# Quantising two weight matrices in 2048-wide pieces instead of 1024-wide ones, with bf16 intermediates

## What is computed

```python
x = x + attention(layernorm(x), Wq, Wk, Wv, Wo, rel_emb)   # 16 heads of 64, relative bias
x = x + ffn(layernorm(x), w1, w2)

def quant_weight(w):                    # the part that the change touches
    s = clip(mean(abs(w)), 1e-5, None)
    return clip(round(w / s), -1, 1) * s
def ffn(x, w1, w2):                     # w1 4096 x 1024, w2 1024 x 4096, float32
    h = gelu(quant_act(x) @ quant_weight(w1).T)
    return quant_act(h) @ quant_weight(w2).T
```

## Time and profile before

| | us |
|---|---|
| median of 3 runs | 9136.47 |
| the profiled execution, its time | 9122.06 |
| its span on the slowest core (core 3) | 9120.5 |
| spans of the 8 cores | 9107.6 to 9120.5 |
| busy in that span: PE / DVE / ACT / POOL | 3183.0 / 2173.7 / 2030.0 / 85.1 |
| the chain that ended last: DMA / DVE / ACT / PE / issue of DMAs by SP | 21% / 19% / 19% / 15% / 12% |

### The profile page before, as it was taken

How to read it: one execution, slowest core, us unless ns; L and a number is a source line. 1 busy time by engine, 2 the same in 40 slices (tenths; PEclk the granted TensorE clock), 3 DMA queues, 4 the chain that set the end, 5 groups by cost and what they waited for, 6 DMA issues and landing times.

```text
span 9120.5 us, 47056 instructions; the slowest of 8 cores (9107.6 to 9120.5 us)
## 1 busy us (share of the span) xinstructions
PE 3183.0 (35%) x12444; PEld 1036.2 (11%) x12444; DVE 2173.7 (24%) x2480; ACT 2030.0 (22%) x2214; POOL 85.1 (1%) x164
## 2 busy tenths in 40 slices
PE   0000014767675100233225225676774000233155
PEld 0000001112121000011112101121211000111022
DVE  0334310000000156266600200000001364366400
ACT  0010102546452010022100004464550000122100
POOL 0000000000000000000000000000000000000000
PEclk9999997889887555666667667898886555666577
DMA  3323222000001400200032122000002301100222
GB/s 69 116 90 124 74 61 52 14 28 14 19 23 51 124 30 28 61 23 23 27 89 75 61 53 42 25 14 19 23 14 78 109 26 46 44 19 23 53 76 74
DMA packets 661831, 459.47 MB, mean 50 GB/s; under 512 B 546242, under 2 KB 579140, under 8 KB 653380
## 3 DMA queue, kind: packets, MB, share of 16 engines
q1 hardware_dynamic: 652868, 447.81, 17.0%
q0 software_dynamic: 8704, 8.66, 0.7%
HBM read 209.23 MB, written 143.79 MB: 39 GB/s over the span
## 4 chain that ended last, share of the span: by engine, by line
DMA 21%; DVE 19%; ACT 19%; PE 15%; SPq 12%; issue 7%; DVEq 5%; ACTq 2%; PEldq 0%; PEld 0%; POOL 0%; POOLq 0%
ACT AR L719 11%; SPq L103 9%; PE PS L970 5%; DMA ARF<-w_in 4%; DVEq L276 3%; PE PS L656 3%; DVE qst_b L290 3%; DVE qst_u L298 2%; DVE qst_c L285 2%; SPq L106 2%; ACT qst_t L933 2%; DVE AR L312 2%; ACT AR L902 2%; DVE stc_mcol L909 2%; DMA lnt<-yat_dram 1%
## 5 line engine op out<-in xcount | busy, mean ns | idle before, releaser
L896 PE MATMUL PS<-AR 128*128 128x512 bf16 x2016 | 507.2, 419 | 2416.8 <-DMA AR<-xq_dram 1541.5
L719 ACT ACTIVATE AR<-PS,neg40c 128x1024 bf16<-128x1024 f32 x1024 | 1140.2, 1113 | 374.4 <-issue 194.0
L970 PE MATMUL PS<-AR 128*128 128x512 bf16 x1984 | 457.0, 390 | 727.8 <-DMA AR<-hq_dram 666.8
L769 DVE RECIPROCAL ARF<-ARF 128x32 f32<-128x32 f32 x16 | 5.6, 353 | 2793.1 <-DMA ARF<-ARF 2793.1
L896 PEld LDWEIGHTS PS<-AR 128*128 128x128 bf16 x2016 | 210.8, 106 | 2713.4 <-issue 2521.9
L604 PE MATMUL PS<-AR 128*128 128x512 bf16 x448 | 142.9, 472 | 968.8 <-DMA AR<-wv_bf 908.3
L700 PE MATMUL PS<-AR 64*128 64x512 bf16 x1024 | 406.3, 397 | 117.9 <-DMA AR<-g_dram 117.9
L730 PE MATMUL PS<-AR 128*65 128x512 bf16 x1024 | 387.8, 379 | 165.1 <-ACTq L92 164.6
L708 PE MATMUL PS<-AR,j_sb 128*128 128x512 bf16 x1024 | 409.2, 400 | 0.0
L704 PE MATMUL PS<-AR 64*128 64x512 bf16 x1024 | 406.6, 397 | 0.0
L712 PE MATMUL PS<-AR,j_sb 128*128 128x512 bf16 x1024 | 399.0, 390 | 0.0
(11 more groups left out here) (111 smaller groups left out, 3536.1 us busy)
## 6 DMA issues: line engine op xcount, KB each, us to landing
ARF<-w_in SPq DMA_DIRECT2D x64, 512.0 KB
ARF<-w_in SPq DMA_DIRECT2D x32, 1024.0 KB
xtile<-x_in SPq DMA_DIRECT2D x64, 512.0 KB
hq_dram<-AR SPq DMA_DIRECT2D x32, 1024.0 KB
AR<-g_dram SPq DMA_DIRECT2D x32, 992.0 KB
x_dram<-x1t SPq DMA_DIRECT2D x32, 512.0 KB
xtile<-x_dram SPq DMA_DIRECT2D x32, 512.0 KB
xtile<-x_dram SPq DMA_DIRECT2D x64, 256.0 KB
```

The source lines that it names most:

```text
L719: E("scalar", lambda S, ewg=ewg, j=j: S.activation(out=ewg[:, 0:1024], in_=PS[:, 1024 * j:1024 * (j + 1)], func=AF.Exp, bias=neg40c[:], sc ...
L896: E("tensor", lambda T, tt=tt, dc=dc, hg=hg: T.matmul(ps[hg], xqT[dc][:, 128 * tt:128 * (tt + 1)], w1qT[dc][:, 512 * hg:512 * (hg + 1)], s ...
L970: T.matmul(ps[bk], hqT[hc][:, 128 * ttl:128 * (ttl + 1)], w2qT[hc][:, 512 * dg:512 * (dg + 1)], start=(hc == 0), stop=False))
```

## The change

In the second pass DVE works on 2048 columns at a time. The two comparisons write bf16 tiles (`qw_b0` and `qw_u0`, or `qw_b1` and `qw_u1`, in turn) instead of float32, and the difference is written in place over the first of them. A piece of w2 is then one part with one store. For w1, whose rows are 1024 long, two row blocks are laid side by side in a buffer (`RB` is 2), with two loads and two stores. This also holds for the first pass over w1: 16 reductions of 2048 instead of 32 of 1024, and `wsum` has one column per pair. A tile of 2048 ones (`ones2k`) is set at the start of the program. All new tiles lie in a part of the buffer `AR` that the stages after the barrier use otherwise. The work of `batch_program` is the same.

```diff
--- before.py
+++ after.py
@@ -262,7 +262,11 @@
         gselch = carve(0, NUM_BUCKETS, 512, F32)
         wchunk = carve(512, 128, 2048, F32)
         wchunk2 = carve(4096, 128, 2048, F32)
-        qst_o2 = carve(50944, 128, 1024)
+        qw_b0 = carve(0, 128, 2048)
+        qw_u0 = carve(2048, 128, 2048)
+        qw_b1 = carve(4096, 128, 2048)
+        qw_u1 = carve(6144, 128, 2048)
+        ones2k = carve(8192, 128, 2048)
 
         PS = es.enter_context(nc.psum_tensor("PS", [128, 4096], F32))
         ps = [PS[:, 512 * i:512 * (i + 1)] for i in range(8)]
@@ -320,6 +324,7 @@
         E("vector", lambda V: V.memset(onesrow[:], 1.0))
         E("vector", lambda V: V.memset(ones_big, 1.0))
         E("vector", lambda V: V.memset(onesr2k, 1.0))
+        E("vector", lambda V: V.memset(ones2k, 1.0))
         v0 = r.inc("vector", "V")
         r.dma("sync", "dS", j_sb[:], jmat_c)
         r.dma("sync", "dS", sel2_sb[:], sel2_c)
@@ -361,17 +366,27 @@
 
         wbufs = (wchunk, wchunk2)
         wbg = {0: None, 1: None}
-        obufs = (qst_o, qst_o2)
+        obufs = ((qw_b0, qw_u0), (qw_b1, qw_u1))
         obg = {0: None, 1: None}
         wq_state = {"g": 0, "o": 0}
 
         def wquant(w_src, w_dst, nrows, ncols, scol):
             CW = 2048 if ncols % 2048 == 0 else 1024
+            RB = 2048 // CW
             nch = nrows // 128
             ncc = ncols // CW
+            n_ig = nch // RB
+
+            def loads(buf, ch, cc):
+                for rb in range(RB):
+                    ld = r.dma("sync", "dS", buf[:, CW * rb:CW * (rb + 1)],
+                               w_src[128 * (ch + rb):128 * (ch + rb + 1),
+                                     CW * cc:CW * (cc + 1)])
+                return ld
+
             E("vector", lambda V: V.memset(wsum[:], 0.0))
             r.inc("vector", "V")
-            for ch in range(nch):
+            for ig in range(n_ig):
                 for cc in range(ncc):
                     bi = wq_state["g"] % 2
                     wq_state["g"] += 1
@@ -379,25 +394,24 @@
                     if wbg[bi]:
                         for sn_, v_ in wbg[bi]:
                             r.wait("sync", sn_, v_)
-                    ld = r.dma("sync", "dS", buf[:, 0:CW],
-                               w_src[128 * ch:128 * (ch + 1), CW * cc:CW * (cc + 1)])
+                    ld = loads(buf, RB * ig, cc)
                     r.wait("vector", "dS", ld)
-                    E("vector", lambda V, CW=CW, buf=buf: V.reduce_sum(
-                        stc["tmp"][:], buf[:, 0:CW], axis=mybir.AxisListType.X,
+                    E("vector", lambda V, buf=buf: V.reduce_sum(
+                        stc["tmp"][:], buf[:, 0:2048], axis=mybir.AxisListType.X,
                         apply_absolute_value=True))
                     VD()
...
                     vv = r.inc("vector", "V")
                     wbg[bi] = [("V", vv)]
             E("vector", lambda V: V.drain())
-            E("vector", lambda V, n=nch: V.reduce_sum(
+            E("vector", lambda V, n=n_ig: V.reduce_sum(
                 wsumt[:], wsum[:, 0:n], axis=mybir.AxisListType.X))
             vv = r.inc("vector", "V")
             r.wait("tensor", "V", vv)
@@ -439,37 +453,35 @@
                     if wbg[bi]:
                         for sn_, v_ in wbg[bi]:
                             r.wait("sync", sn_, v_)
-                    ld = r.dma("sync", "dS", buf[:, 0:CW],
-                               w_src[128 * ch:128 * (ch + 1), CW * cc:CW * (cc + 1)])
+                    ld = loads(buf, RB * ig, cc)
                     r.wait("scalar", "dS", ld)
-                    E("scalar", lambda S, CW=CW, buf=buf: S.activation(
-                        out=buf[:, 0:CW], in_=buf[:, 0:CW], func=AF.Identity,
+                    E("scalar", lambda S, buf=buf: S.activation(
+                        out=buf[:, 0:2048], in_=buf[:, 0:2048], func=AF.Identity,
                         bias=zeroc[:], scale=rscol[:]))
                     sc = r.inc("scalar", "S")
                     r.wait("vector", "S", sc)
-                    for sub in range(CW // 1024):
-                        ssl = slice(1024 * sub, 1024 * (sub + 1))
-                        oi = wq_state["o"] % 2
-                        wq_state["o"] += 1
-                        ob = obufs[oi]
-                        if obg[oi] is not None:
-                            r.wait("vector", "dS", obg[oi])
-                        E("vector", lambda V, buf=buf, ssl=ssl: V.scalar_tensor_tensor(
-                            out=qst_b[:], in0=buf[:, ssl], scalar=0.5,
-                            in1=ones_big, op0=ALU.is_ge, op1=ALU.mult))
-                        E("vector", lambda V, buf=buf, ssl=ssl: V.scalar_tensor_tensor(
-                            out=qst_u[:], in0=buf[:, ssl], scalar=-0.5,
-                            in1=ones_big, op0=ALU.is_lt, op1=ALU.mult))
-                        VD()
-                        E("vector", lambda V, ob=ob: V.tensor_tensor(
-                            out=ob[:], in0=qst_b[:], in1=qst_u[:], op=ALU.subtract))
-                        vv = r.inc("vector", "V")
-                        r.wait("sync", "V", vv)
+                    oi = wq_state["o"] % 2
+                    wq_state["o"] += 1
+                    qb, qu = obufs[oi]
+                    if obg[oi] is not None:
+                        r.wait("vector", "dS", obg[oi])
+                    E("vector", lambda V, buf=buf, qb=qb: V.scalar_tensor_tensor(
+                        out=qb[:], in0=buf[:, 0:2048], scalar=0.5,
+                        in1=ones2k, op0=ALU.is_ge, op1=ALU.mult))
+                    E("vector", lambda V, buf=buf, qu=qu: V.scalar_tensor_tensor(
+                        out=qu[:], in0=buf[:, 0:2048], scalar=-0.5,
+                        in1=ones2k, op0=ALU.is_lt, op1=ALU.mult))
+                    VD()
+                    E("vector", lambda V, qb=qb, qu=qu: V.tensor_tensor(
+                        out=qb[:], in0=qb[:], in1=qu[:], op=ALU.subtract))
+                    vv = r.inc("vector", "V")
+                    r.wait("sync", "V", vv)
+                    for rb in range(RB):
                         sv = r.dma("sync", "dS",
-                                   w_dst[128 * ch:128 * (ch + 1),
-                                         CW * cc + 1024 * sub:CW * cc + 1024 * (sub + 1)],
-                                   ob[:])
-                        obg[oi] = sv
+                                   w_dst[128 * (RB * ig + rb):128 * (RB * ig + rb + 1),
+                                         CW * cc:CW * (cc + 1)],
+                                   qb[:, CW * rb:CW * (rb + 1)])
+                    obg[oi] = sv
                     wbg[bi] = [("S", sc), ("V", vv)]
 
         wquant(w1_in, w1q_dram, HID, D, s1col)
```

More of the change, by code:

```diff
@@ L389, in wquant @@
                     if cc == 0:
-                        E("vector", lambda V, ch=ch: V.tensor_tensor(
-                            out=wsum[:, ch:ch + 1], in0=stc["tmp"][:], in1=zeroc[:],
+                        E("vector", lambda V, ig=ig: V.tensor_tensor(
+                            out=wsum[:, ig:ig + 1], in0=stc["tmp"][:], in1=zeroc[:],
                             op=ALU.add))
                     else:
-                        E("vector", lambda V, ch=ch: V.tensor_tensor(
-                            out=wsum[:, ch:ch + 1], in0=wsum[:, ch:ch + 1],
+                        E("vector", lambda V, ig=ig: V.tensor_tensor(
+                            out=wsum[:, ig:ig + 1], in0=wsum[:, ig:ig + 1],
                             in1=stc["tmp"][:], op=ALU.add))
```

## The result

The changed kernel takes 8992.04 us (median of 8 runs, 8980.67 to 9012.25) against 9137.63 us for the kernel before in the same comparison (8 runs, 9127.91 to 9150.8). The ratio is 0.9841 with a 95% interval of 0.9831 to 0.9852: 146 us, or 1.6%, less.

The account below looks back on a forecast made before the run. Chains of waits in `wquant`, not PE or bandwidth, were taken as the bound. Gains of 24 (w1's first pass), 56.7 and 51.8 us (second passes) less 4 us added make 128 us: 9136.5 - 128 = 9008 us, range 8980 to 9052 us.

Parts of the forecast that it names:

- four serial steps: First and second passes over w1 and w2 in `wquant`, 798 us in all, each a repeated step with a fixed order.
- reload legs: Second pass, from a store's issue to the next scaling by ACT; forecast 7.2 us per piece for both matrices.
- First pass over w1: Loads in 16 overlapping pairs instead of 32 in sequence, 5.25 us a step; 24 us gained.
- low end of 5.20 us: First pass over w1: lower bound for a pair of loads, from w2's 1 MB load; the upper was 6.80 us.
- Compute leg: Second pass, a piece's scaling by ACT and three DVE instructions until its store is issued; forecast 8.24 us.
- counting bytes: Second pass: the bf16 difference of 2048 columns costs 1.23 us, like the old instruction on operands of the same bytes.
- What was added: Fill of ones at the start, extra store issue after w1, larger last store of w2; together 4 us lost.
- the payment by elements: Rival on the second pass's difference: 2.29 us instead of 1.23 us, 34 us less gain, 9042 us; chance 0.12.
- the pairs that don't overlap: Rival on w1's paired DMAs: first pass gains nothing, its reload leg is 8.3 us, 9049 us in all; chance 0.08.
- The lower clock: Rival on the attention stage: starting some 128 us earlier, it gets a lower clock; 9320 us in one case; chance 0.03.
- the 15 us that the prediction set as a sign of being wrong: Prediction wrong if the two batch items take more than 15 us other than 4025 and 4038 us.
- The cheap second store: Rival on the second pass: second store costs only its issue, reload leg 6.72 us, 14 us more gain, 8994 us; chance 0.05.

## Why the prediction was right, and where it was off

The reading of the bound held: four serial steps, each made of legs that add up. Three parts were tried alone in the old kernel, and by the start of the next stage they gave 36 us for the wait inside a piece of w2, 32 us for bf16 (64 x 0.534 = 34 us by its rows) and 27 us for the pairs in w1's first pass. That is 95 of the 144 us. The other 49 us are by subtraction what the wider pieces save in the second pass; no run tried these alone, and that the parts add up is assumed. The legs fit it: the reload legs of w1 alone give 31 x 4.07 - 15 x 6.41 = 30 us of them.

First pass over w1: 5.08 us a step (5.03 us over the eight cores), a little below even the low end of 5.20 us; the pair overlaps fully. The gain was 26.5 us and not 24 us.

Compute leg: 8.21 and 8.28 us against 8.24 us (8.29 and 8.34 us over all pieces, which loses 2 us). The value that was chosen between far ends, 1.23 us for the difference, is 1226 ns. But the reason given, counting bytes, is wrong, and the right value by it was luck: with one float32 operand in three the instruction takes the full 2292 ns. It is fast where all three operands are bf16, and not where one input is float32. The Trainium skill (VectorE: DVE Perf Modes, "The perf-mode tier table (the rule you actually need)") gives 1224 ns for 2048 bf16 elements and 2293 ns in float32. The 1226 ns of this trace agree with the first.

Reload leg: this is the term that was mis-sized. The prediction took 7.2 us for both matrices, from w2's old leg of 6.27 us plus a second store at 0.93 us. Over all pieces and cores the leg is 7.02 us for w2 and 6.41 us for w1. The second 256 KB of stores cost 7.02 - 6.33 = 0.69 us in w2. In w1, 512 KB of stores cost 1.43 us (the run without them), where 256 KB cost 4.07 - 3.38 = 0.69 us before (3.38 us is the first pass's step over the eight cores), so the second cost 0.74 us. And w1's leg does not start from w2's 6.27 us: without stores it is 4.97 us, and its stores go to contiguous memory, which is 0.35 to 0.45 us cheaper. With w1's own step and cost from the rows, 5.20 + 2 x 0.77 = 6.7 us, the sum would have been 7 us nearer. Of the 16 us by which the forecast was off, 15 x 0.79 = 12 us come from this leg in w1 and 15 x 0.18 = 3 us in w2; the compute legs take 2 us back; the rest, 3 us, is in the first pass and in what was added.

What was added cost 4 us on core 3 as forecast, but spread otherwise, and 2.6 us over the eight cores. The start lost 3.4 us (2.4 us over the eight cores): the fill takes the forecast 1.76 us, and with the step before it SP's first store is issued 2.14 us later (6.98 instead of 4.84 us). The larger last store cost nothing.

Of the rivals, the payment by elements is refuted by the 1226 ns, and the pairs that don't overlap by the 5.08 us step. The lower clock is refuted by the attention stage: its exponential takes 1114 ns with 374.8 us of idle time before it in all, against 1113 ns and 374.4 us, on the slowest core of each execution. Over the eight cores the batch items moved by 5.5 and -5.3 us. On core 3 they took 4018.7 and 4022.7 us instead of 4025.1 and 4037.7 us; the second just reaches the 15 us that the prediction set as a sign of being wrong, within the spread of single cores (4020 to 4042 us after) and towards faster. The cheap second store has the number that came nearest: its 6.72 us is the mean of 6.41 and 7.02 us, and its 8994 us is nearer to 8992 us than the forecast. Its mechanism does not hold: a second store costs 0.7 us and not the 0.45 us of its issue, and what makes the mean small is w1's cheaper loads and stores.

## What to carry to other kernels

Where a stage is a chain of waits, price each leg by its own rows, and take the matrix's own rows even if another's look alike. When a wait for a shared counter means a wait for every transfer issued so far, larger pieces only make the rounds fewer: here 1.6%, with bf16 and the pairs in it. On top of that, issuing loads ahead with a semaphore for each buffer and a third buffer for the round trip gave 5.0% in all, and only then did an engine set the pace (DMA in the first pass, DVE in the second). Count buffers as round trip over the time of the slowest engine: 15.1 us over 6.1 us is 2.5, and three were enough where two were not.

## What was not expected of the hardware

Stores of the same 512 KB cost the leg 0.35 to 0.45 us more when they go to rows of 4 KB at a pitch of 8 KB than to contiguous memory (means of the eight cores). Splitting each of w2's DMAs in two made the first pass slower, 5.44 against 5.22 us for 1 MB. The subtraction with one float32 and one bf16 input gained nothing from its 2-byte operands: 2292 ns for 2048 columns, as a float32 comparison of that length.
